# Attention scores of an 8-core transformer layer: the even head's table term moves from VectorE to a float32 product on TensorE

## The reference, cut to what matters

```python
xn = layernorm(x)                               # x: (4, 4096, 1024) float32
q, k, v = heads(xn @ Wq + bq), ...              # 16 heads of 64
bias = slope[h] * (pos_k - pos_q)               # ALiBi, float32
scores = einsum('bhqd,bhkd->bhqk', q, k) * 0.125 + bias
ctx = softmax(scores) @ v
x = x + ctx @ Wo + bo + ffn(xn)                 # ffn: 1024 -> 4096 -> 4096 -> 4096 -> 1024
```

## Time and profile before

| | |
|---|---|
| Median of the runs shown (2) | 5020.01 us (5011.16 and 5028.86) |
| The profiled execution's own time | 4999.97 us |
| Its span, slowest core (core 5) | 4998.4 us |
| Spans of the eight cores | 4957.8 to 4998.4 us |
| Mean granted clock of the cores | 0.844 to 0.860 |
| TensorE matmul busy, weight load busy | 74%, 30% of the span |
| VectorE, ScalarE, GpSimd busy | 23%, 19%, 3% |

### The profile page before, as it was taken

One profiled execution on the slowest core, in us unless ns is written; L12 is line 12 of the kernel. 1 busy time (PEld: TensorE's weight loads), 2 busy tenths in 40 slices (PEclk: granted clock), 3 DMA queues, 4 the chain that ended last, 5 costly groups with the idle time before them and its releaser, 6 DMA issues.

```text
span 4998.4 us, 41656 instructions; the slowest of 8 cores (4957.8 to 4998.4 us)
## 1 busy us (share of the span) xinstructions
PE 3710.3 (74%) x15436; PEld 1509.2 (30%) x15436; DVE 1154.5 (23%) x1371; ACT 970.1 (19%) x1398; POOL 158.0 (3%) x239
## 2 busy tenths in 40 slices
PE   2436544596555655644899999999579999999968
PEld 1223201141111111111344444444234444444424
DVE  4454454534444344332110000000011000000001
ACT  1110022104555655530110000000001100000000
POOL 1000000100000000000000000000000000000000
PEclk9857655695767767677999999999789999999989
DMA  4333000320000000015344443444444344344452
GB/s 132 121 101 101 14 18 28 99 70 22 29 37 37 24 32 37 28 56 150 77 68 76 76 76 68 76 76 76 93 105 72 68 76 76 68 76 77 76 98 74
DMA packets 110675, 345.66 MB, mean 69 GB/s; under 512 B 5905, under 2 KB 51089, under 8 KB 92049
## 3 DMA queue, kind: packets, MB, share of 16 engines
q0 software_dynamic: 64640, 201.34, 22.2%
q1 hardware_dynamic: 45842, 141.65, 8.5%
HBM read 498.16 MB, written 29.36 MB: 106 GB/s over the span
## 4 chain that ended last, share of the span: by engine, by line
PE 67%; DVE 11%; DMA 10%; ACT 7%; issue 4%; DVEq 1%; SPq 0%; POOL 0%; ACTq 0%; POOLq 0%
PE PSA L705 9%; PE PSA L689 9%; PE PSB L705 9%; PE PSB L689 9%; PE PSA L671 5%; PE PSB L671 4%; DVE AR L931 4%; PE PSB L600 4%; ACT AR L761 4%; ACT AR L757 3%; DMA AR<-x_own 3%; PE PSB L603 3%; PE PSA L587 2%; PE PSA L611 2%; DVE AR L918 2%
## 5 line engine op out<-in xcount | busy, mean ns | idle before, releaser
L757 ACT ACTIVATE AR<-AR,p2a 128x512 bf16<-128x512 f32 x528 | 380.4, 721 | 962.8 <-DVE AR L918 811.3
L600 PE MATMUL PSB<-AR 128*65 128x512 bf16 x526 | 261.9, 498 | 386.1 <-ACT AR L761 386.1
L918 DVE SCALAR_TENSOR_TENSOR AR<-PSA,AR 128x512 f32<-128x512 f32 x528 | 361.8, 690 | 589.6 <-PE PSA L589 554.0
L980 DVE TENSOR_TENSOR AR<-PSA,s3b 128x1024 f32<-128x1024 f32 x8 | 9.8, 1224 | 1997.3 <-PE PSA L722 1997.3
L705 PE MATMUL PSA<-AR 128*128 128x512 bf16 x2048 | 451.6, 382 | 18.1 <-DMA AR<-h2sl 18.1
L689 PE MATMUL PSA<-AR 128*128 128x512 bf16 x2048 | 447.2, 379 | 3.4 <-DVE AR L966 3.4
L705 PE MATMUL PSB<-AR 128*128 128x512 bf16 x2048 | 447.2, 379 | 0.0
L689 PE MATMUL PSB<-AR 128*128 128x512 bf16 x2048 | 447.2, 379 | 0.0
L761 ACT ACTIVATE AR<-PSA,p2b 128x512 bf16<-128x512 f32 x528 | 353.2, 669 | 0.0
L611 PE MATMUL PSA<-AR,ones 1*128 1x512 f32 x120 | 122.4, 1121 | 263.0 <-DVE AR L931 263.0
L671 PE MATMUL PSA<-AR 128*128 128x512 bf16 x1024 | 231.5, 385 | 85.3 <-DMA AR<-xno_d 54.7
(11 more groups left out here) (93 smaller groups left out, 2400.3 us busy)
## 6 DMA issues: line engine op xcount, KB each, us to landing
AR<-h1sl POOLq DMA_DIRECT2D x64, 1024.0 KB, 8.4
AR<-h2sl POOLq DMA_DIRECT2D x64, 1024.0 KB, 8.3
AR<-U SPq DMA_DIRECT2D x12, 2240.0 KB, 8.0
AR<-x_own SPq DMA_DIRECT2D x32, 512.0 KB, 4.5
AR<-x_seq SPq DMA_DIRECT2D x32, 512.0 KB, 3.5
AR<-xnf_d SPq DMA_DIRECT2D x8, 2048.0 KB, 10.0
AR<-w1sl POOLq DMA_DIRECT2D x16, 1024.0 KB, 10.1
AR<-w2sl POOLq DMA_DIRECT2D x16, 1024.0 KB, 14.3
```

The lines of the kernel that those rows point to most:

```text
L600: pe.matmul(ctxA(gi2)[0:65, :], vt[:, kt2, 2 * g2["pi"], :], eT[:, (pe2 % 2) * 512:(pe2 % 2) * 512 + 512], start=f2, stop=l2)
L757: sc.activation(eT[:, (e % 2) * 512:(e % 2) * 512 + 512], tsc[:, e % 2, :], AF.Exp, bias=p2a[:, P * 32 + kt: P * 32 + kt + 1], scale=1.0). ...
L918: ve.scalar_tensor_tensor(tsc[:, e % 2, :], PSA[:, (e % 2) * 1024:(e % 2) * 1024 + 512], 0.125, ub[:, off:off + 512], ALU.mult, ALU.add).t ...
```

## The change

The table term of head A is no longer added by VectorE. TensorE adds it in PSUM: behind A's score product, which now leaves its accumulation open, stands a float32 product of the 128x128 identity `idn` with 512 columns of `ub`, accumulated into the same bank; then B's scores. `exp` of A reads PSUM with scale 0.125, as B's does. The table is stored times 8, since it is now scaled together with the scores. Line 918 and its count `s_vst` are gone; what waited for `s_vst` waits for `s_qk`, and the wait for the table's load stands on TensorE, ahead of a group's first score product.

```diff
@@ sync: the table's load @@
                     if gi > 0:
-                        sy.wait_ge(s_vst, EV_START[gi])
+                        sy.wait_ge(s_qk, EV_START[gi])
@@ gpsimd: weights of the second half, and Wo @@
-                    gp.wait_ge(s_vst, EV_HALF0_END)
...
-                gp.wait_ge(s_vst, NEV)
+                gp.wait_ge(s_qk, NEV)
@@ tensor @@
                         elif ki == 1:
                             pe.wait_ge(s_cp, 2 * gi)
+                        if ki == 0:
+                            pe.wait_ge(s_ub, 16 * (gi + 1))
...
+                        off = 3968 - kt * 128
                         pe.matmul(scoreA(e), kA, qf[0:64, q0:q0 + 512],
-                                  start=True, stop=True, tile_position=(0, 0))
+                                  start=True, stop=False, tile_position=(0, 0))
+                        pe.matmul(scoreA(e), idn[:, :], ub[:, off:off + 512],
+                                  start=False, stop=True)
                         pe.matmul(scoreB(e), kB, qf[64:128, q0:q0 + 512],
                                   start=True, stop=True,
                                   tile_position=(64, 0)).then_inc(s_qk, 1)
@@ scalar @@
                         sc.wait_ge(s_qk, e + 1)
-                        sc.wait_ge(s_vst, e + 1)
...
+                        sA = PSA[:, (e % 2) * 1024:(e % 2) * 1024 + 512]
                         sc.activation(eT[:, (e % 2) * 512:(e % 2) * 512 + 512],
-                                      tsc[:, e % 2, :], AF.Exp,
+                                      sA, AF.Exp,
                                       bias=p2a[:, P * 32 + kt: P * 32 + kt + 1],
-                                      scale=1.0).then_inc(s_exa, 1)
+                                      scale=0.125).then_inc(s_exa, 1)
@@ vector @@
-                    for ki, kt in enumerate(g["kts"]):
-                        e = n_ev
-                        ve.wait_ge(s_qk, e + 1)
-                        if ki == 0:
-                            ve.wait_ge(s_ub, 16 * (gi + 1))
-                        if e >= 2:
-                            ve.wait_ge(s_exa, e - 1)
-                        off = 3968 - kt * 128
-                        ve.scalar_tensor_tensor(tsc[:, e % 2, :],
-                                                PSA[:, (e % 2) * 1024:(e % 2) * 1024 + 512],
-                                                0.125, ub[:, off:off + 512],
-                                                ALU.mult, ALU.add).then_inc(s_vst, 1)
-                        n_ev += 1
+                    n_ev += len(g["kts"])
@@ make_inputs @@
-            eps = T.astype(np.float64) - np.float64(SLOPES32[h]) * dgrid
-            m[f"U{h}"] = eps.astype(f32)
+            eps8 = 8.0 * (T.astype(np.float64) - np.float64(SLOPES32[h]) * dgrid)
+            m[f"U{h}"] = eps8.astype(f32)
```

## The result

The changed kernel takes 5486.74 us (median of 11 executions) against 5020.01 (median of 10 of the kernel before). The ratio is 1.0965, with a 95% interval of 1.0912 to 1.1018: about 9.7% slower. The profiled execution's slowest core spans 5476.8 us, against 4998.4.

A forecast was written before the change was run, and what follows sets the result against it. Before, a chain (scores, line 918, `exp`) bound attention with no engine full; after, TensorE. Longer distances between endings, leftover groups and first loads sum to +374 us on 5000, 5374; the median lies 20 higher: 5395 us, range 5200 to 5590.

The forecast's parts named there:

- The signs that it named: Profile after: A's and B's scores over a microsecond apart, AV starts 2.2 us apart, TensorE waiting some 170 us for loads.
- (a): The new float32 product on TensorE: four passes and 0.10, 0.96 us at 2.4 GHz; 1.86 at 1.2.
- (b): Order around the product: four turns between 64-row and 128-row products per event, 0.09 us each at 2.4 GHz.
- Rival 1: Products on TensorE pack better, turns and the 0.10 costing nothing: pace 1.78, about 5205 us; chance 0.14.
- Rival 2: The identity's float32 weight loads on TensorE stand exposed: about 5560 to 5580 us; chance 0.14.
- (c): Attention's pace: TensorE sets it at 2.19 us per event; ScalarE and VectorE have slack, removed VectorE work gives nothing more.
- floor of 1.78: Attention's pace per event: were products free, it could not fall below 1.78 us.
- (d): The table's load comes ahead of each group's ending: 4.4 us plus the load per group, waits about 170 us.
- The slow time after an ending: TensorE starts each group at 1.2 GHz after an ending: 4.3 us, or 1.07 events, per group.
- Rival 3: The clock stays at 1.2 GHz in attention, 4.02 us per event: about 6230 us; chance 0.08.
- Rival 4: Not slower: the float32 product passes once (0.22 us), an event takes 1.45: about 4970 us; chance 0.06.

The follow-up runs named there:

- e2_noprod: The changed kernel without the identity product, the table still loaded and waited for but not added to head A's scores: span 4847.8 us, ratio 0.9614.
- e5_order: The changed kernel with the float32 product moved behind B's scores: span 5190.9 us, ratio 1.0347 to the kernel before.
- e1_dbuf: The changed kernel with a second buffer for the table, its load issued one group earlier: span 5285.3 us, ratio 1.0521 to the kernel before.
- e4_waitonly: The kernel before with TensorE waiting for the table ahead of a group's first scores, VectorE still adding it: span 5121.3 us, ratio 1.0248.
- e3_bf16: The changed kernel with the product as one bf16 pass in the same place: span 5480.0 us, ratio 1.0928 to the kernel before.
- e8_bf16_dense: e3_bf16 with 128 columns of `qf` (dense values) in place of the identity: span 5485.7 us, one execution.
- e7_bf16_order: e3_bf16 with the bf16 product moved behind B's scores: span 4908.3 us, one execution.

## Why the prediction was right

The forecast was 5395 us, in a range of 5200 to 5590; measured 5486.74. Against its own base, 5374 was summed and the profiled execution spans 5476.8. The signs that it named came: A's and B's scores 1.38 us apart, a pace of 2.24, 164 us of waits for the table. The sum is short by 103 us of a loss of 478, and between the endings it is short everywhere in the same direction: by 22 us over groups 0 to 14, 16 over 16 to 19, 56 over 19 to 30. So it wasn't saved by errors that cancel. Point by point:

- *(a), the float32 product.* 0.96 us of the array and a turn of 0.09 were forecast, 1.06 together was found. It is the largest part of the loss: e2_noprod takes 629 us off, with the scores side by side again.
- *(b), the turns.* Shown: 0.10 each in the timeline after; e5_order takes away two and a pass and gains 0.43 of pace. Rival 1, that turns cost nothing, is out.
- *Rival 2, the identity's loads exposed in full (pace about 2.6),* is out: both loads end 0.30 us after the product's start, while the first of its two instructions runs, and the pace is 2.24. The prediction had named for it the rule of the Trainium skill ("TensorE: Matmul & The Clock Gate", The mechanism) that a weight load runs beside a matmul in flight only where their row groups differ. Here that does not hold between products of full height: the float32 product's second load and the load for B's AV (L607, 1632.90) both run under a matmul on the same rows. At each change between half and full height the timeline agrees with it. The same section of the Trainium skill names a second case, a load into a background weight buffer, which the prediction left out; no run here shows whether that is what happens.
- *(c), who sets the pace.* TensorE, as forecast, at 2.24 against 2.19. 0.05 in 458 events is 23 us of the missing 103. That removed VectorE work gives nothing more under this bound was right, but e2_noprod shows what it would give without it: 0.45 us per event, by estimate about 240 us in 528, which the change has and loses. The prediction's floor of 1.78 is misnamed, "were products free": the 1.72 in it is eight passes, so 1.78 is the pace with free turns. Without the product the same chain gives (1.83 + 0.43 + 0.09 + 0.22)/2 = 1.29, and e2_noprod has 1.24.
- *(d), the table's wait.* Forecast "about 170 us" of waits; the profile has 164, e1_dbuf takes off 191 with what follows from them, and e4_waitonly shows 124 for the wait alone. From the last scores' end to the first reciprocal, with a load of 8 us, 12.4 was forecast; at the ending shown above it is 12.8 (the last B starts at 1587.07 and takes the array 0.22, the reciprocal starts at 1600.07).
- *The slow time after an ending.* This term was mis-sized. I took 4.3 us from a stretch of full-width products. In the changed kernel it is 10.2 us on average over the eight cores (groups 19 to 30), and single groups have up to 16:

```profile
1710.00:1727.00 17.00, 16.35 (x25) 0.50 0.00 0
1727.00:1790.00 63.00, 60.54 (x162) 1.00 0.03 9
```

  TensorE's matmuls are busy 16.35 of 17 us and the clock is still 0.50. Of the 5.9 us more, an event at 4.07 in place of 2.24 loses 45%: 2.7 us per group, some 55 in the twenty longer groups. With the 23 that is most of the 103, by estimate; 16 us are the stages ahead, which the change doesn't touch: the first scores start at 561.8 on this core and at 545.9 on the slowest core of before, where the cores spread from 540.6 to 553.3. The trace of before could have warned: over the same twelve endings its clock rises 23 us after the ending on average, and up to 59. That slow time was already in the distances between its endings, and the change shortened it; this is the clock of 0.70 that became 0.82.
- *Rival 3* (the clock stays low, since float32 passes of an identity might count for nothing) had its direction wrong. With float32 passes the clock does rise; with one bf16 pass in the same place it never does in attention (e3_bf16), and a dense stationary operand changes nothing (e8_bf16_dense).
- *Rival 4* needed a product under 0.45 us. A cheap product alone (e3_bf16) would not have done it either; it takes the order too (e7_bf16_order, 4908.3, though that kernel ran once).

## What to carry to other kernels

Work taken off an engine with slack and put on TensorE is priced by the array's passes: a 128x512 float32 addition that took VectorE 0.69 us took the array the time of four passes and a little more, split a pair of half-height products that had run side by side, and cost 1.0 us. When a buffer's last reader moves to another engine, ask what stands behind the new wait: here the load, hidden behind an ending before, came to stand ahead of it. Before giving such a change up, try the place of the new product, its type and a second buffer; together they turned 9.7% slower into 4.8% faster.

## What the runs showed of the hardware that I had not expected

TensorE can run for 81 us without waiting for another engine and still be held at 1.2 GHz: in e3_bf16 the clock was 0.50 over the 1490 us of half 1's attention, with 2.61 us per event, all of them passes and turns, while e7_bf16_order, with TensorE busy for less of the time and A and B side by side, was granted 0.81. The changed kernel lies between, with rises 4 to 16 us after an ending. For the bf16 pass, its place decides between the two clocks. What in that order the clock answers to is not settled by these runs: A and B apart, four turns in place of two, or something that goes with them. Nor is it shown why the float32 product in the same place lets it rise.

A change between 64-row and 128-row products costs 0.09 to 0.10 us at the upper clock and 0.10 to 0.14 at the lower. A float32 product of 512 columns takes the array 0.96 us at the upper clock, with both loads hidden under it.
